# A new order of pieces with four places in a step, scores of one step in nine sent by pairs through the ring, and sums of values on column tiles

## The chip, the core and the metric

One core of a Trainium2 chip runs the whole program. The metric is the device time in microseconds (us), median of the runs shown. TensorE (PE), VectorE (DVE), ScalarE (ACT), GpSimd (POOL) and the DMA queue of SyncE (SP) work side by side and meet only at semaphores.

## The reference

The input x is 8 batches x 1024 tokens x 256 features, in fp32. Each batch goes through

```python
h = layernorm(x) * (1 + ca) + sa
x = x + ga * attention(h)        # 16 heads of 16 features
h = layernorm(x) * (1 + cb) + sb
x = x + gb * spikes(relu(h @ W_fc.T) ** 2 @ W_proj.T)   # 1024 hidden features, 5 LIF steps
```

The attention has two softmaxes. The scores (1024 x 1024 for a head) are cut into blocks of 128 keys; a first softmax runs inside each block with the causal mask, and a second softmax runs over the whole row of the first one's results, in which the masked entries count as zero and so give exp(0) = 1. The kernel therefore adds to each output the sum of the values of all later key blocks: this is the "sum of values" (pieces BH and BT below).

## The kernel before

**Steps.** The heads of a batch are taken four at a time (a group g), and a group in nine units of four PSUM banks, one for each head. The main loop has one step for each unit: 8 batches x 4 groups x 9 units = 288 steps and 14 more to drain. 36 steps make a period, which does the attention of one batch. Below, position p is the step's number modulo 36, and u = p modulo 9 the unit. Every engine runs the same steps in its own instruction order, written out in `step(n)` of that engine.

In step n PE does, in this order: `products` (second softmax times values, of step n - 7, L800), `sum_unit` (sums of the exponentials of step n - 1, L790), two `one_over_sums` (the inverse sums of step n - 5 spread over the partitions, L829), and the four `scores` (one for each head, L775, with a mask at L778), between which lie the tiles of maxima of the next group (`maxima`, L750 and L753), the pieces and the quanta. Step u = 0 has also `mixed_products`.

**PSUM.** Two banks `score0` and `score1` serve in turn the scores of each head, the pieces and the turned maxima: an item waits until the item before it in its bank has been taken away, mostly by ACT. Two double banks, the ring, serve in turn the two `one_over_sums` of a step, the maxima and the outputs; DVE takes these. One bank holds the sums, one the products.

**ACT** in a step: the second exponential of step n - 6 (L1046), every third step a logarithm and an exponential of sums (L1052, L1056), then the first exponentials of the four heads (L1041) with the evacuations of pieces (`take`) between them. **DVE**: every third step of nine an addition into `o_t` (L1196), two products with the inverse sums (L1180), every third step the inverse (L1184, L1186), then the maxima (L1158), after the last of a group a cast and a subtraction (L1172, L1174), layer norm statistics (L1132). After that PE turns the maxima (L763), ACT copies them (L1032), and SP loads them beside the queries with four DMAs (L554). **POOL**: split of the inverse sums (L1488 to L1494), split of queries and keys into three bf16 parts (L1454 to L1458), squares (L1467), LIF counts (L1475 to L1481), and the second half of each layer norm. **SP** stores the parts (L535), and loads the stacked parts of a whole group (L546) when step u = 0 is issued, in one order for all of it.

**Pieces.** Everything else of a batch is cut into pieces with a step and a place each, in hand-written tables: `FRONT` for the next batch (T1: transposes of the normalised input, QK: queries or keys, V: values, BH and BT: sum of values), `BACK` for the batch before (AT, O, T2, F1), `QUANTA` for single products with W_proj (L732, two instructions each). A piece at place 0 follows the score of head 0, at place 1 that of head 3. `TILES_AT` says how many maxima tiles a unit holds (three in each of u = 1 to 6).

**BH** does seven products of 8 columns of weights with 272 columns of values, all into the same 8 partitions of PSUM (L697, 14 instructions as fp32 takes two), ACT copies 8 x 272 numbers (L998), and **BT** turns them with four transposes (L702).

Of the kernel before, what the change touches and what calls it, by code (L numbers as in the profile page):

```python
# [5 lines left out]
F32 = mybir.dt.float32  # L6
# [7 lines left out]
P = 128  # L14
# [40 lines left out]
LAG_R, LAG_E, LAG_P = 5, 6, 7  # L55
LAST = NUNIT + 14
# [7 lines left out]
for _h in range(QH):  # L64
# [7 lines left out]
TILES_AT = {1: 3, 2: 3, 3: 3, 4: 3, 5: 3, 6: 3}  # L72
# [9 lines left out]
FRONT = {(2, 1): ('T1', 0), (1, 0): ('T1', 1), (1, 1): ('T1', 2), (5, 0): ('T1', 3), (3, 1): ('QK', 0), (5, 1): ('QK', 1), (6, 0): ('QK', 2), (13, 0): ('QK', 3), (15, 0): ('QK', 4), (16, 1): ('QK', 5), (17, 0): ('QK', 6), (15, 1): ('V', 0), (19, 1): ('QK', 7), (24, 0): ('V', 1), (21, 1): ('V', 2), (29, 0): ('V', 3), (30, 0): ('BH', 0), (31, 0): ('BT', 0)}  # L82
BACK = {(8, 0): ('AT', 0), (8, 1): ('AT', 1), (9, 0): ('AT', 2), (12, 0): ('AT', 3), (10, 0): ('O', 0), (11, 0): ('O', 1), (12, 1): ('O', 2), (14, 0): ('O', 3), (18, 0): ('T2', 0), (18, 1): ('T2', 1), (20, 1): ('T2', 2), (24, 1): ('T2', 3), (19, 0): ('F1', 0), (20, 0): ('F1', 1), (21, 0): ('F1', 2), (23, 0): ('F1', 3), (26, 1): ('F1', 4), (27, 0): ('F1', 5), (27, 1): ('F1', 6), (28, 0): ('F1', 7), (32, 0): ('F1', 8), (32, 1): ('F1', 9), (33, 0): ('F1', 10), (35, 0): ('F1', 11), (38, 0): ('F1', 12), (39, 0): ('F1', 13), (40, 0): ('F1', 14), (40, 1): ('F1', 15)}
# [3 lines left out]
QUANTA = {22: (3, 1, 0, 0), 23: (0, 0, 1, 1), 25: (1, 0, 2, 0), 26: (0, 2, 3, 0), 28: (0, 1, 0, 1), 29: (1, 1, 1, 2), 31: (2, 1, 1, 2), 32: (1, 0, 1, 0), 34: (1, 1, 1, 0), 35: (0, 1, 1, 2), 37: (1, 1, 0, 1), 38: (2, 0, 3, 0), 41: (1, 2, 0, 2), 43: (2, 2, 0, 0), 44: (1, 0, 1, 1), 36: (0, 0, 0, 1), 42: (0, 0, 2, 0), 30: (0, 0, 1, 0), 24: (0, 0, 1, 1), 45: (0, 0, 0, 1), 40: (1, 0, 0, 0)}  # L87


NEAR = {(39, 0): ("F1", 12), (39, 1): ("F1", 13), (41, 0): ("F1", 14), (41, 1): ("F1", 15)}  # L90
NEAR_QUANTA = {36: (0, 0, 0, 1), 37: (1, 1, 0, 1), 38: (2, 0, 3, 0), 42: (2, 2, 2, 2), 43: (2, 2, 2, 2)}
LATE = {(2, 0): ("AT", 0), (2, 1): ("AT", 1), (4, 0): ("O", 0), (4, 1): ("O", 1), (8, 0): ("AT", 2), (8, 1): ("AT", 3),
        (9, 0): ("T2", 0), (9, 1): ("T2", 1), (10, 0): ("O", 2), (10, 1): ("O", 3), (11, 0): ("F1", 0), (11, 1): ("F1", 1),
        (12, 0): ("F1", 2), (12, 1): ("F1", 3), (13, 0): ("F1", 4), (13, 1): ("F1", 5)}
# [4 lines left out]
    (2, 0): ("V", 0, 2), (2, 1): ("V", 0, 3), (6, 1): ("BH", 0, 0), (7, 1): ("BT", 0, 0),  # L99
    (10, 0): ("T1", 1, 0), (10, 1): ("T1", 1, 1), (11, 0): ("T1", 1, 2), (11, 1): ("T1", 1, 3),  # L100
# [5 lines left out]
FIRST[25, 0] = ("BH", 1, 0)  # L106
FIRST[26, 0] = ("BT", 1, 0)
# [9 lines left out]
def placed(n):  # L117

    out = [None, None]
    b, at = divmod(n, PERIOD)  # L120
    for k in range(2):
# [96 lines left out]

RING_NO = {}
for _k in range(BEGIN_TILES):  # L220
    RING_NO["m", 0, _k] = len(RING_NO)
for _n in range(LAST):
    if 0 <= _n - LAG_R < NUNIT:
        for _k in range(2):
            RING_NO["r", _n - LAG_R, _k] = len(RING_NO)
    for _g, _k in tiles_of(_n):
        RING_NO["m", _g, _k] = len(RING_NO)
    if turned_out(_n):
        RING_NO["o", turned_out(_n)[0], int(turned_out(_n)[1][0] > 0)] = len(RING_NO)

# [34 lines left out]

def score_slots():
# [3 lines left out]
    for n in range(LAST):  # L270
        p = placed(n)
        st = [("st", n, hh) for hh in range(QH)] if n < NUNIT else [None] * QH
        turn = ("turn", *turn_of(*turns(n))) if turns(n) else None
        begin = [p[0], st[0]] if piece_first(n) else [st[0], p[0]]
        steps.append([*begin, st[1], st[2], st[3], p[1], turn] if late_turn(n) else [*begin, st[1], turn, st[2], st[3], p[1]])
# [22 lines left out]
C_ID, C_MQ, C_MT, C_SEL, C_DS, C_U, C_AB, C_OH = 0, 128, 256, 384, 390, 428, 444, 448  # L298
# [3 lines left out]
def constants():  # L302
# [12 lines left out]
    c[:, C_U:C_U + NB - 1] = 1.0  # L315
    for j in range(NB):
        for row in (KROWS + 2 * j, KROWS + 2 * j + 1):
            c[row, C_OH + P * j:C_OH + P * (j + 1)] = 1.0
# [32 lines left out]
def build(nc, x, wqT, wkT, wvT, woT, bq, bk, bv, bo, wfcT, wprojT, cT, wmod, consts, out):  # L351
# [4 lines left out]
    with ExitStack() as ctx:  # L356
# [34 lines left out]
        b_out = sb("b_out", [P, 2 * D], BF16)  # L391
# [122 lines left out]

        block = ctx.enter_context(nc.Block())
# [3 lines left out]
        def _(sp):  # L519
# [123 lines left out]
        def _(pe):  # L643
# [11 lines left out]
            def ring_slot(*item):  # L655
                no = RING_NO[item]
                if no >= 2:
                    pe.wait_ge(ring_free, no - 1)
# [8 lines left out]
            def tokens_by(ps, src, n, w, bias=None):  # L667

                if bias is not None:
                    pe.matmul(ps, one[:, :].to_broadcast([P, P]), bias[:, :], start=True, stop=False, skip_group_check=True)  # L670
# [6 lines left out]
            def piece(item):  # L677
# [15 lines left out]
                elif kind == "BH":  # L693

                    piece_done(pe, "V", r, 3)
                    for j in range(1, NB):
                        mm = pe.matmul(ps[own_rows, 0:H * VW], u_ind[:, NB - 1 - j:2 * NB - 1 - j], v1[:, r % 2, j, :, :].rearrange("p h c -> p (h c)"),  # L697
# [870 lines left out]
```

## Time and profile before

| | |
|---|---|
| time, median of 3 runs | 2356.11 us (2353.27 to 2359.1) |
| profiled execution, its own time | 2358.39 us |
| span of its instructions | 2356.6 us |
| PE busy | 2206.2 us (94%) |
| DVE busy | 1753.1 us (74%) |
| ACT busy | 1541.6 us (65%) |
| POOL busy | 1137.6 us (48%) |
| mean granted PE clock | 0.990 |

The span lies 1.8 us under the execution's own time. Busy time is the union of an engine's instructions; a PE instruction counts as busy from its start to the modelled end of its result, so that neighbours overlap: the distance between two starts says what an instruction costs.

### The profile page before, as it was taken

To read this page: it belongs to the slowest core of one execution; us is meant where nothing else is said; L and a number is where in the kernel's file an instruction comes from. 1 tells how busy PE (TensorE), PEld (TensorE's weight loads), DVE (VectorE), ACT (ScalarE), POOL (GpSimd) and SP (SyncE) were. 2 spreads that over 40 slices of the span, in tenths; PEclk is the share of its full clock that TensorE was granted. 3 is DMA by queue.
4 is the path that set the end of the run, shared out by engine and by line. 5 is a ranking of instruction groups with operands and counts; after the bars stand their busy time and mean duration, and the time that the engine had idled before them with its cause. 6 is when DMAs were issued, how large, how long until landed. Compare 5 with 4: busy or idle time off the path is not lost.

```text
span 2356.6 us, 46649 instructions
## 1 busy us (share of the span) xinstructions
PE 2206.2 (94%) x19164; PEld 1247.1 (53%) x19164; DVE 1753.1 (74%) x2115; ACT 1541.6 (65%) x2157; POOL 1137.6 (48%) x1070
## 2 busy tenths in 40 slices
PE   6889889999999999999998999999999999989988
PEld 4434334455555555455554655545555555545557
DVE  7786887768787676886778777776877767788466
ACT  2477677766667667676777766776666766667741
POOL 3153133545755456644576257653576544443630
PEclk9999999999999999999999999999999999999999
DMA  5233122311122113121133102231022211101000
GB/s 188 62 109 94 48 55 71 94 48 33 54 68 84 52 35 90 41 68 52 35 90 95 47 20 59 66 108 48 8 70 77 84 35 46 39 19 29 6 27 25
DMA packets 114064, 140.20 MB, mean 59 GB/s; under 512 B 8648, under 2 KB 86760, under 8 KB 113856
## 3 DMA queue, kind: packets, MB, share of 16 engines
q1 hardware_dynamic: 113856, 137.23, 20.5%
q8 instruction: 155, 2.54, 0.5%
q14 instruction: 53, 0.43, 0.1%
HBM read 74.26 MB, written 58.74 MB: 56 GB/s over the span
## 4 chain that ended last, share of the span: by engine, by line
PE 77%; DVE 10%; ACT 5%; POOL 4%; issue 2%; DMA 1%; SPq 0%; ACTq 0%; POOLq 0%
PE pv L800 11%; PE ring L750 9%; PE sums L790 9%; PE score L775 9%; PE score L720 9%; PE sums L732 8%; PE score L673 5%; PE score L688 4%; DVE e L1180 4%; PE ring L829 4%; DVE negmax L1158 3%; PE ring L753 2%; PE score L778 2%; PE score L664 2%; ACT e L1041 2%
## 5 line engine op out<-in xcount | busy, mean ns | idle before, releaser
L1041 ACT ACTIVATE e<-score 128x512 f32<-128x512 f32 x1152 | 672.7, 595 | 372.8 <-PE score L778 207.6
L1180 DVE TENSOR_TENSOR e<-ring,e 128x1024 f32<-128x1024 f32 x576 | 681.2, 1224 | 278.1 <-PE ring L829 277.5
L1158 DVE TENSOR_REDUCE negmax<-ring 128x8 f32<-128x1024 f32 x576 | 681.7, 1219 | 150.7 <-PE ring L753 139.4
L1046 ACT ACTIVATE e<-e 128x2048 f32<-128x2048 f32 x288 | 548.6, 1905 | 4.9 <-DVE e L1180 4.9
L775 PE MATMUL score<-q_st,k_st 112*128 112x512 bf16 (+3 forms) x1536 | 459.5, 330 | 57.3 <-ACT e L1041 22.5
L750 PE MATMUL ring<-k_st,q_st 96*128 96x512 bf16 (+3 forms) x1664 | 387.5, 318 | 39.1 <-DVE e L1180 18.1
L1488 POOL TENSOR_SCALAR r_p<-r_b,ab 128x256 bf16<-128x256 f32 x96 | 89.6, 934 | 544.5 <-DVE r_b L1186 544.5
L800 PE MATMUL pv<-e,v 128*17 128x512 f32 (+3 forms) x3072 | 314.4, 497 | 1.3 <-DVE o_t L1196 1.3
L790 PE MATMUL sums<-e,d_ones 128*32 128x256 f32 x4608 | 305.1, 383 | 1.4
L775 PEld LDWEIGHTS score<-q_st,k_st 112*128 112x128 bf16 x1536 | 147.9, 97 | 248.9 <-issue 122.7
L1467 POOL TENSOR_TENSOR gT<-gT 128x512 f32<-128x512 f32 x112 | 117.2, 1051 | 331.5 <-ACT gT L1014 331.5
L732 PE MATMUL sums<-w_proj,gT 128*128 128x256 f32 x896 | 259.3, 394 | 8.1 <-POOL gT L1467 3.7
L720 PE MATMUL score<-hT,w_fc 128*128 128x256 f32 x1024 | 244.2, 383 | 2.7 <-ACT e L1041 1.4
L790 PEld LDWEIGHTS sums<-e,d_ones 128*32 128x32 f32 x4608 | 147.6, 111 | 179.4 <-issue 96.9
L750 PEld LDWEIGHTS ring<-k_st,q_st 96*128 96x128 bf16 x1664 | 150.1, 99 | 147.4 <-DVE negmax L1158 42.4
L753 PE MATMUL ring<-mask_q,id_b 128*128 128x128 bf16 x1024 | 221.5, 221 | 0.0
L720 PEld LDWEIGHTS score<-hT,w_fc 128*128 128x128 f32 x1024 | 189.7, 190 | 33.2 <-ACT e L1041 6.3
L778 PE MATMUL score<-id_b,mask_q 128*128 128x128 bf16 x1024 | 192.3, 220 | 0.0
L732 PEld LDWEIGHTS sums<-w_proj,gT 128*128 128x128 f32 x896 | 148.5, 191 | 38.7 <-DVE r_b L1184 6.6
L1479 POOL TENSOR_SCALAR below<-n 128x512 bf16<-128x512 f32 x104 | 154.9, 1490 | 7.4
L1014 ACT ACTIVATE gT<-score 128x512 f32<-128x512 f32 x112 | 66.9, 597 | 123.4 <-PE score L720 123.4
L753 PEld LDWEIGHTS ring<-mask_q,id_b 128*128 128x128 bf16 x1024 | 100.3, 98 | 53.6 <-issue 3.5
(147 smaller groups left out, 2574.9 us busy)
## 6 DMA issues: line engine op xcount, KB each, us to landing
q_st<-q_parts SPq DMA_DIRECT2D x31, 768.0 KB, 5.9
k_st<-k_parts SPq DMA_DIRECT2D x31, 768.0 KB, 8.6
q_parts<-qk_p SPq DMA_DIRECT2D x30, 384.0 KB, 2.6
k_parts<-qk_p SPq DMA_DIRECT2D x28, 384.0 KB, 2.6
x_in<-in_x SPq DMA_DIRECT2D x8, 1024.0 KB, 5.7
q_parts<-qk_p SPq DMA_DIRECT2D x30, 256.0 KB, 2.9
x_res<-in_x SPq DMA_DIRECT2D x30, 256.0 KB, 4.1
k_parts<-qk_p SPq DMA_DIRECT2D x28, 256.0 KB, 2.9
```

Source lines behind the costliest of these rows:

```text
L720: mm = pe.matmul(ps[:, HALF * i:HALF * i + HALF], w_fc[:, k, P * f:P * f + P], (last_h if r == LB else hT2)[:, k, HALF * c:HALF * c + HALF ...
L732: mm = pe.matmul(sums[:, HALF:HALF + D], gT[:, f, P * i:P * i + P], w_proj[:, f, :], start=(n > NUNIT and f == 0), stop=(f == NF - 1), ski ...
L750: mm = pe.matmul(slot[:, c:stop], q, k_st[0:KROWS, g % 2, hh, c + shift:stop + shift], start=True, stop=not own, skip_group_check=True)
L753: mm = pe.matmul(slot[:, diag:diag + P], id_b[:, :], mask_q[:, :], start=False, stop=True, skip_group_check=True)
L775: mm = pe.matmul(slot[:, c:c + qb - qa], k_st[0:KROWS + MROWS, g % 2, hh, P * j:P * j + P], q_st[0:KROWS + MROWS, g % 2, hh, qa:qb], start ...
L778: mm = pe.matmul(slot[:, c:c + P], mask_q[:, :], id_b[:, :], start=False, stop=True, skip_group_check=True)
L790: mm = pe.matmul(sums[32 * hh:32 * hh + 32, 0:HALF], d_ones[:, 2 * TRI - 1 - row:2 * TRI + 31 - row], e[:, m % ES, hh, HALF * c:HALF * c + ...
L800: mm = pe.matmul(pv[32 * hh:32 * hh + VW, qa - at:qb - at], v1[:, b % 2, j, QH * g + hh, :], e[:, m % ES, hh, c:c + qb - qa], start=start, ...
L1041: act.activation(e[:, n % ES, hh, :], score[SCORE_SLOT["st", n, hh][0]][:, :], ACT.Exp, scale=DK ** -0.5).then_inc(e1_done, 1)
L1046: act.activation(v, v, ACT.Exp).then_inc(e2_done, 1)
L1158: dve.tensor_reduce(negmax[:, hh:hh + heads, at:at + NB // heads], slot[:, :].rearrange("p (h a n) -> p h a n", h=heads, n=P), AX_X, ALU.m ...
L1180: dve.tensor_tensor(v, ring[no % 2][:, :].rearrange("p (i n) -> p i n", i=2), v, ALU.mult).then_inc(ring_free, 1)
```

## The change

- `placed` gives four places, one behind the score of each head, and `FRONT`, `BACK` and `QUANTA` are new. `TILES_AT` has two tiles at u = 3 and four at u = 4.
- In the 31 steps with u = 0 that hold no tiles (`paired`) the scores of heads 0 and 1 go into one double bank of the ring, those of heads 2 and 3 into the other, and ACT takes each with one exponential of 1024 columns. Places 0 and 1 then lie ahead of the scores, place 2 between the pairs, place 3 behind them. The two score banks serve only pieces there.
- BH writes its seven products to four groups of 32 partitions in turn, with 32 columns of weights; ACT copies 128 x 272 numbers into `o_t`; BT is 16 small products (17 columns of weights, 8 of data) instead of four transposes. DVE's write to `o_t` waits for BT.
- The bias of the output projection is made once and read twice, which takes one DVE instruction off the start.

```diff
-TILES_AT = {1: 3, 2: 3, 3: 3, 4: 3, 5: 3, 6: 3}
+TILES_AT = {1: 3, 2: 3, 3: 2, 4: 4, 5: 3, 6: 3}
-FRONT = {(2, 1): ('T1', 0), (1, 0): ('T1', 1), (1, 1): ('T1', 2), (5, 0): ('T1', 3), (3, 1): ('QK', 0), (5, 1): ('QK', 1), (6, 0): ('QK', 2), (13, 0): ('QK', 3), (15, 0): ('QK', 4), (16, 1): ('QK', 5), (17, 0): ('QK', 6), (15, 1): ('V', 0), (19, 1): ('QK', 7), (24, 0): ('V', 1), (21, 1): ('V', 2), (29, 0): ('V', 3), (30, 0): ('BH', 0), (31, 0): ('BT', 0)}
+FRONT = {(0, 0): ('T1', 0), (0, 1): ('T1', 1), (5, 2): ('T1', 2), (1, 3): ('T1', 3), (0, 3): ('QK', 0), (5, 3): ('QK', 1), (6, 0): ('QK', 2), (13, 3): ('QK', 3), (15, 0): ('QK', 4), (15, 2): ('QK', 5), (17, 0): ('QK', 6), (16, 3): ('V', 0), (19, 3): ('QK', 7), (24, 0): ('V', 1), (18, 2): ('V', 2), (29, 0): ('V', 3), (35, 0): ('BH', 0), (35, 3): ('BT', 0)}
-BACK = {(8, 0): ('AT', 0), (8, 1): ('AT', 1), (9, 0): ('AT', 2), (12, 0): ('AT', 3), ..., (12, 1): ('O', 2), ..., (24, 1): ('T2', 3), ..., (35, 0): ('F1', 11), ...}
+BACK = {(9, 0): ('AT', 0), (8, 0): ('AT', 1), (12, 3): ('AT', 2), (12, 0): ('AT', 3), ..., (13, 0): ('O', 2), ..., (22, 3): ('T2', 3), ..., (33, 2): ('F1', 11), ...}
-QUANTA = {..., 25: (1, 0, 2, 0), 26: (0, 2, 3, 0), ..., 29: (1, 1, 1, 2), 31: (2, 1, 1, 2), ..., 42: (0, 0, 2, 0), 43: (2, 2, 0, 0), 44: (1, 0, 1, 1), 45: (0, 0, 0, 1), 30: (0, 0, 1, 0), ...}
+QUANTA = {..., 25: (1, 2, 1, 1), 26: (1, 0, 2, 0), ..., 29: (0, 1, 0, 0), 31: (2, 3, 2, 0), ..., 42: (0, 0, 1, 0), 43: (1, 1, 1, 0), 44: (2, 1, 1, 1), 30: (0, 0, 0, 3), ...}
+def paired(n):
+    return n % NU in PAIRED and n < NUNIT and not tiles_of(n)
...
                 elif kind == "BH":
                     piece_done(pe, "V", r, 3)
                     for j in range(1, NB):
-                        mm = pe.matmul(ps[own_rows, 0:H * VW], u_ind[:, NB - 1 - j:2 * NB - 1 - j], v1[...], start=(j == 1), stop=(j == NB - 1))
+                        own = slice(32 * (j % 4), 32 * (j % 4) + 32)
+                        mm = pe.matmul(ps[own, 0:H * VW], u_ind[:, NB - 1 - j:NB + 31 - j], v1[...], start=(j <= 4), stop=(j >= 4), skip_group_check=True)
                 elif kind == "BT":
                     for g in range(NQ):
-                        mm = pe.transpose(ps[:, NB * g:NB * g + NB], suf_t[...], id_f[own_rows, own_rows])
+                        for hh in range(QH):
+                            mm = pe.matmul(ps[32 * hh:32 * hh + VW, NB * g:NB * g + NB], suf_p[:, QH * g + hh, 0:VW], eight[:, :], start=True, stop=True, skip_group_check=True)
...
+                if paired(n):
+                    if p[1]:
+                        piece(p[1])
+                    for item in single[0]:
+                        quantum(n, *item)
+                    scores(n, 0)
+                    scores(n, 1)
...
+                    if p[2]:
+                        piece(p[2])
...
+                    scores(n, 2)
+                    scores(n, 3)
+                    if p[3]:
+                        piece(p[3])
...
+            def paired_exp(n, pair):
+                no = RING_NO["s", n, pair]
+                act.wait_ge(ring_ready, no + 1)
+                act.activation(e[:, n % ES, 2 * pair:2 * pair + 2, :], ring[no % 2][:, :].rearrange("p (i n) -> p i n", i=2), ACT.Exp, scale=DK ** -0.5).then_inc(e1_done, 2)
```

## Rows read from the trace of the kernel before

**Rows 1.** Windows: span, busy us of PE, PEld, DVE, ACT, POOL, clock, DMA.

```profile
1145.83:1426.43 280.60, 270.66 (x2391) 153.96 (x2391) 211.71 (x247) 192.82 (x271) 157.16 (x146) 1.00 0.21 60
...
1237.16:1273.02 35.86, 32.60 (x278) 16.08 (x277) 33.19 (x39) 24.46 (x34) 25.21 (x24) 1.00 0.13 42
1378.72:1395.33 16.61, 16.61 (x129) 7.99 (x129) 13.84 (x17) 9.80 (x16) 3.83 (x5) 1.00 0.05 17
```

**Rows 2.** Groups by line: busy us, mean ns, idle before, releasers.

```profile
L1158 DVE TENSOR_REDUCE negmax<-ring 128x8 f32<-128x1024 f32 x576 | 681.7, 1219 | 150.7 <-PE ring L753 139.4 <-PE ring L750 8.7
L1180 DVE TENSOR_TENSOR e<-ring,e 128x1024 f32<-128x1024 f32 x576 | 681.2, 1224 | 278.1 <-PE ring L829 277.5
L1041 ACT ACTIVATE e<-score 128x512 f32<-128x512 f32 x1152 | 672.7, 595 | 372.8 <-PE score L778 207.6 <-PE score L775 142.9
L1046 ACT ACTIVATE e<-e 128x2048 f32<-128x2048 f32 x288 | 548.6, 1905 | 4.9 <-DVE e L1180 4.9
L775 PE MATMUL score<-q_st,k_st 112*128 112x512 bf16 (+3 forms) x1536 | 459.5, 330 | 57.3 <-ACT e L1041 22.5 <-ACT qk_p L992 18.8 <-ACT m_sb L1032 9.4
```

**Rows 3.** Timeline, PE, position 0: around the score of head 2.

```profile
1148.64 0.22 PE L778 MATMUL score<-id_b,mask_q 128*128 128x128 bf16 x1
1149.45 0.38 PE L775 MATMUL score<-q_st,k_st 112*128 112x512 bf16 x1 [0.58 <-ACT e L1041]
```

**Rows 4.** Timeline, PE, positions 18 and 27: around the same kind of wait.

```profile
1288.31 0.22 PE L778 MATMUL score<-id_b,mask_q 128*128 128x128 bf16 x1
1288.87 0.38 PE L775 MATMUL score<-q_st,k_st 112*128 112x512 bf16 x1 [0.35 <-ACT hT L974]
...
1357.08 0.22 PE L778 MATMUL score<-id_b,mask_q 128*128 128x128 bf16 x1
1357.88 0.38 PE L775 MATMUL score<-q_st,k_st 112*128 112x512 bf16 x1 [0.58 <-ACT e L1041]
```

**Rows 5.** Timeline, DVE, position 0: the products that free the ring.

```profile
1147.68 2.35 DVE L1180 TENSOR_TENSOR e<-ring,e 128x1024 f32<-128x1024 f32 x2 [0.17 <-PE ring L829]
```

**Rows 6.** Chain of waits at positions 30 and 31: start, us, what.

```profile
1381.29 3.31 PE score L697 x14
...
1389.96 0.34 PE score L702 x4
```

**Rows 7.** Chain of waits: two `products`, one of 384 and 128 columns, one of 512.

```profile
1195.57 0.99 PE pv L800 x16
...
1203.56 0.98 PE pv L800 x8
```

**Rows 8.** Timeline, POOL: first split of QK1, last split of QK2.

```profile
1195.53 1.17 POOL L1454 TENSOR_TENSOR qk_p<-qk_f,qk_p 128x512 bf16<-128x512 f32 x1 [1.24 <-ACT qk_p L992]
...
1210.81 1.18 POOL L1458 TENSOR_TENSOR qk_p<-qk_f,qk_p 128x512 bf16<-128x512 f32 x1
```

**Rows 9.** Timeline, SP, and from the DMA view the last one's landing.

```profile
1212.02 2.76 SPq L535 DMA_DIRECT2D k_parts<-qk_p  x3
1214.82 2.39 SPq L554 DMA_DIRECT2D q_st<-m_sb  x4
1217.88 0.48 SPq L546 DMA_DIRECT2D k_st<-k_parts  x1
...
k_st<-k_parts SPq DMA_DIRECT2D x1, 768.0 KB, 8.8
```

**Rows 10.** Timeline, PE, position 10: the first tile of maxima.

```profile
1226.84 0.22 PE L750 MATMUL ring<-k_st,q_st 96*128 96x128 bf16 x1
```

**Rows 11.** Timeline, PE and DVE, position 16: the turn of the maxima.

```profile
1273.02 0.61 PE L763 MATMUL score<-id_b,maxp 128*64 128x128 bf16 x8 [1.53 <-DVE maxp L1174]
...
1271.25 1.62 DVE L1174 TENSOR_TENSOR maxp<-negmax,maxp 128x168 bf16<-128x168 f32 x1
```

**Rows 12.** Timeline, PE, position 17: a score behind a QK piece.

```profile
1283.91 0.34 PE L775 MATMUL score<-q_st,k_st 112*128 112x384 bf16 x1 [1.02 <-ACT qk_p L992]
```

**Rows 13.** Timeline, DVE, the start: the bias, made twice.

```profile
38.85 2.55 DVE L1352 TENSOR_TENSOR b_out<-e 3x256 bf16<-3x256 f32 x2
```

More of the change, by code:

```diff
@@ L55 @@
 LAG_R, LAG_E, LAG_P = 5, 6, 7
+PAIRED = (0,)
 LAST = NUNIT + 14
@@ L117, in placed @@
 def placed(n):
-    out = [None, None]
+    out = [None] * 4
     b, at = divmod(n, PERIOD)
-    for k in range(2):
+    for k in range(4):
         if b == 0 and (at, k) in FIRST:
@@ L216, in turned_out, with last_turned, last_summed @@
     return None
+PIECE_STEP = {piece: n for n in range(LAST) for piece in placed(n) if piece}
+def last_turned(n):
+    done = [turned_out(k)[0] for k in range(n) if turned_out(k)]
+    return done[-1] if done else None
+def last_summed(n):
+    done = [r for r in range(B) if PIECE_STEP["BT", r, 0] < n]
+    return done[-1] if done else None
+def paired(n):
+    return n % NU in PAIRED and n < NUNIT and not tiles_of(n)
 RING_NO = {}
@@ L227 @@
         RING_NO["m", _g, _k] = len(RING_NO)
+    if paired(_n):
+        for _k in range(2):
+            RING_NO["s", _n, _k] = len(RING_NO)
     if turned_out(_n):
         RING_NO["o", turned_out(_n)[0], int(turned_out(_n)[1][0] > 0)] = len(RING_NO)
+RING_ITEM = list(RING_NO)
+FREE_NO = {item: k for k, item in enumerate(item for item in RING_ITEM if item[0] != "s")}
 def turns(n):
@@ L263, in piece_first @@
     return mixed(n) or n == max(BEGIN_AT) + 1
+ST_NO = [QH * sum(not paired(k) for k in range(n)) for n in range(NUNIT)]
 def score_slots():
@@ L271, in score_slots @@
         p = placed(n)
-        st = [("st", n, hh) for hh in range(QH)] if n < NUNIT else [None] * QH
+        st = [("st", n, hh) for hh in range(QH)] if n < NUNIT and not paired(n) else [None] * QH
         turn = ("turn", *turn_of(*turns(n))) if turns(n) else None
+        if paired(n):
+            steps.append([p[0], p[1], turn, p[2], p[3]])
+            continue
         begin = [p[0], st[0]] if piece_first(n) else [st[0], p[0]]
-        steps.append([*begin, st[1], st[2], st[3], p[1], turn] if late_turn(n) else [*begin, st[1], turn, st[2], st[3], p[1]])
+        steps.append([*begin, st[1], p[1], *([] if late_turn(n) else [turn]), st[2], p[2], st[3], p[3], *([turn] if late_turn(n) else [])])
     steps.append(TAIL)
@@ L315, in constants @@
     c[:, C_U:C_U + NB - 1] = 1.0
+    for i in range(NB):
+        c[i::32, C_8 + i] = 1.0
     for j in range(NB):
@@ L669, in tokens_by @@
                 if bias is not None:
-                    pe.matmul(ps, one[:, :].to_broadcast([P, P]), bias[:, :], start=True, stop=False, skip_group_check=True)
+                    pe.matmul(ps, one[:, :].to_broadcast([P, P]), bias[:, :].unsqueeze(1).to_broadcast([P, 2, D]), start=True, stop=False, skip_group_check=True)
                 for i in range(2):
@@ L879, in step @@
             def step(n):
-                first, second = placed(n)
+                p = placed(n)
                 single = quanta(n)
@@ L901, in step @@
                     scores(n, 0)
-                if first and not piece_first(n):
-                    piece(first)
+                if p[0] and not piece_first(n):
+                    piece(p[0])
                 for item in single[0]:
@@ L923, in step @@
                     maxima(*at[2])
-                if second:
-                    piece(second)
+                if p[3]:
+                    piece(p[3])
                 if 3 in at:
@@ L1077, in step @@
                 b, s = divmod(n, PERIOD)
-                first, second = placed(n)
+                p = placed(n)
                 t = n // TRI - 1
@@ L1195, in take_products @@
                     dve.wait_ge(ring_ready, RING_NO["o", g - 1, 0] + 1)
+                if half == 0 and last_summed(n) is not None:
+                    piece_full(dve, "BT", last_summed(n), 0)
                 dve.tensor_tensor(o_t[:, BANK * half:BANK * half + BANK].rearrange("p (i n) -> p i n", n=P),
@@ L1382, in step @@
                     invert(t)
-                first, second = placed(n)
-                if first and first[0] == "O":
-                    take_output(first)
+                p = placed(n)
+                for item in p[:2]:
+                    if item and item[0] == "O":
+                        take_output(item)
                 tiles = tiles_of(n)
@@ L1388, in step @@
                     maxima(g, k)
-                if second and second[0] == "O":
-                    take_output(second)
+                for item in p[2:]:
+                    if item and item[0] == "O":
+                        take_output(item)
                 if turned_out(n):
```

192 lines of the change are left out of this document (131 added, 61 removed).

## The prediction

> **What bounds the kernel now.** I read the busy times first: PE 270.7 of the 280.6 us of a period, DVE 211.7, ACT 192.8, POOL 157.2 [rows 1]. PE paces the whole, yet not alone: since all 36 positions repeat to 0.01 us from batch to batch, I went through one period start by start. Summing the distances between PE starts and setting against them what each kind of instruction takes when nothing holds it leaves about 26 us per period beyond the work, of which 11 are small gaps of 0.1 us (some three a step, an estimate that I take as unavoidable), and 15 are real waits. The change can give back only these 15 and whatever PE work it removes. Where the 15 lie:
>
> - Positions with u = 0: 1.2, 1.0, 1.2 and 1.3 us. The four scores share two banks, so the third waits for the exponential of the first: from the mask at 1148.64 to the next score at 1149.45 are 0.81 us where 0.06 would do [rows 3]; positions 18 and 27 show 0.56 and 0.80 [rows 4], each with smaller ones behind.
> - Positions 12 to 16: 4.6 us up to the turn of the maxima. From the start of step 12 to the turn are 35.86 us, and DVE is busy in 33.2 of them [rows 1]: two products and three tiles of 1.22 us a step [rows 2], with outputs, statistics and the cast on top. The turn waits 1.5 us for DVE's last subtraction [rows 11].
> - A score that needs the bank of a QK piece, which ACT empties with two instructions: 1.0 us at position 17 [rows 12], the like at 6 and 13, and 1.2 us at 16 behind the copy of the turned maxima.
> - Positions 33 to 35: 1.8 us, DVE again.
>
> **BH and BT.** Fourteen instructions take 3.31 us on PE [rows 6], 0.236 each, as all write the same 8 partitions. On four groups of 32 partitions at most two products (four instructions) share a group: 4 x 0.236 = 0.94. The nearest row says that groups do overlap: `products` takes 0.98 us for eight instructions of 512 columns over four such groups [rows 7]. That saves 2.4 us; the bounds are 0 (no overlap) and 2.5 (3.31 / 4). BT was 0.34 us for four transposes [rows 6]; now it is 32 instructions. Sixteen instructions, eight of 384 and eight of 128 columns, take 0.99 us, and eight of 512 take 0.98 [rows 7]; at three quarters of that the first eight cost 0.74, which leaves 0.25 for the other eight, 0.031 each, with 17 columns of weights like BT's. 32 x 0.031 = 1.0 us. From the transposes (0.34 / 4 = 0.085 each) it would be 2.7; the low bound is the 0.34 of before. I take 1.0, since the 17 columns of weights are the same. Net 1.7 us for a batch; the bounds are a gain of 2.5 (full overlap, BT as before) and a loss of 2.4 (no overlap, BT at 2.7). Six batches have it on PE's path: 10.2 us. The first period computes two more in steps where DVE sets the pace, of which I count half: 1.7 us. Sum 11.9 us.
>
> TensorE's floor for small matmuls speaks against BT: the Trainium skill ("TensorE: Matmul & The Clock Gate", section "Wait — 56ns, not 53.3ns?") gives about 62 ns for a matmul when the sequencer decodes in software, and about 25 ns otherwise. With 62 BT would take 2.0 us and the net saving shrink from 1.7 to 0.7 us a batch; the 0.031 worked out from the products [rows 7] disagrees with 62 and fits 25.
>
> **The paired scores.** Their exponential of 1024 columns: 595 ns for 512 and 1905 for 2048 [rows 2] give 0.853 ns a column, so 1.03 us, 0.16 less than two. ACT is not the bound, so this counts only through waits. What counts is when the ring is free: the first pair needs DVE's first product (ends near 1148.9), the second pair the second (1150.03) [rows 5]. At position 0, PE would reach the scores at 1148.1; T1 0 and T1 1 (0.44 each) now lie ahead of them and carry it to 1149.0, so the first pair runs at once, to 1149.6; the second waits until 1150.1, 0.5 us; QK0 follows behind it. Waits 1.2 before, 0.6 after. At 18, V2 (1.7 us) lies between the pairs and covers the second product: 1.2 to 0.2. At 27, F1 5 (1.7 us) lies ahead: 1.3 to 0.1. At 9 only AT 0 is there: some 0.5 remains, and the next `sum_unit` waits for the exponential of the second pair.
>
> **Positions 6 to 10: a chain that PE doesn't set.** The first split of QK1 starts at 1195.53, at the head of step 6, and POOL works without a gap to 1211.99 through it, the last LIF count, the gate and residual, the inverse sums and QK2 [rows 8]. Behind it SP, in its own order, issues QK2's stores, the four loads of maxima, then the stacks, the last at 1217.88, landing 8.8 us later at 1226.7; PE's first tile from that stack starts at 1226.84 [rows 9, 10]. So this stretch of 31.3 us is as long as POOL, SP and DMA make it, and PE stands at its edge already. The change takes 0.9 us of PE work out of it (AT 2 leaves, one quantum net leaves) and moves QK1's evacuation 0.4 us later against the head of step 6. The queue's content is the same. Nothing is won by the pairs at 9, and the waits grow from 2.0 to 3.1.
>
> **Positions 12 to 16.** DVE's load there is the same: one tile moves from 12 to 13, O2 too. AT 2 fills 0.4 us of the wait. Against it, V0 (one evacuation) changes places with QK5, and QK5 now lies ahead of the last two tiles, which so reach DVE close together; walked through step by step, DVE ends its subtraction about 1 us later. Waits 4.6 to 5.1. POOL's QK5 split now comes directly behind QK4's, and SP stores QK5 ahead of the loads of maxima: these land some 3 us before the scores of 18 need them, so I count nothing; without that cover every us would count one. The waits behind the turn at 16 and behind QK6 at 17 stay at 2.3.
>
> **Positions 29 to 35.** BH, which DVE used to catch up, leaves position 30: 3.3 us less, while DVE has 6.5 us of work in it (two products, two tiles, inverse, two statistics) and then four tiles. It was busy in 13.8 of 16.6 us of steps 30 and 31 [rows 1]; these shrink to about 15. Walked through, the ring holds PE 1.4 us at 30: 0.2 to 1.5. F1 11 between the pairs of tiles at 33 and the earlier square at 35 give 1.8 to 1.0. Other positions (2 and 4 tiles at 3, 4, 21, 22; more quanta at 25) 0.2 to 0.4.
>
> **Sum for a period.** Before 1.2 + 2.0 + 4.6 + 2.3 + 1.2 + 1.3 + 0.2 + 1.8 + 0.2 = 14.8; after 0.6 + 3.1 + 5.1 + 2.3 + 0.2 + 0.1 + 1.5 + 1.0 + 0.4 = 14.3. That is 0.5 x 6 = 3 us in six periods. The seven paired steps of the first and last period give 0.6 each, 4 us. The bias is costed at nothing: one of two DVE instructions of together 2.55 us goes [rows 13], but the first tiles wait for their stacks' DMAs there; at most 1.3. In all 11.9 + 3 + 4 = 19 us off the profiled execution's 2358.4, which is 2.3 above the median: 2356 - 19 = 2337 us. As my walks round every wait up, I put the forecast at 2336.
>
> **The rivals.**
> 1. *The order fits* (0.2). Neither DVE nor the stack chain binds as I have it: then the waits of 6 to 16 fall by what the pairs save and those of 29 to 31 stay at 0.2: 14.8 - 4 = 10.8 a period, 24 + 4 + 11.9 = 40 us, 2316. For it: POOL is idle in much of the period; against it: DVE's 33.2 of 35.9.
> 2. *Small matmuls and no overlap eat BH's gain* (0.1). BT at 2.7 us leaves nothing of it: 7 us off, 2349; without overlap too, a loss of 2 us a batch, 2362.
> 3. *The pairs stall PE as much as the banks did* (0.1): the first pair waits for DVE, the next sums for a whole exponential of 1.03. Then only BH's 11.9 remain less 3 to 8 us: 2348 to 2353.
> 4. *Slower* (0.1). The store of QK5 ahead of the loads of maxima: QK5's split takes three POOL instructions of 1.17 and its three stores 2.76 [rows 8, 9], 6.3 us in a row ahead of the loads, of which my walk finds room for all and 3 us more. If the maxima land later than that by x, every period loses x: from x = 19 / 6 = 3.2 us the gain is gone, and with x = 5 it is 30 us lost, 2367.
>
> **How the numbers follow.** Forecast's own case 0.5, with 2325 to 2346. The measurement can tell about 0.3% (7 us) from no change. Faster than 2349: 0.5 + 0.2 + half of the rivals 2 and 3 = 0.78. Within 7 us: 0.11. Slower: 0.11. The range from 2308 to 2356 holds the own case, rivals 1 and 3 and half of 2.
>
> **What would show it.** BH near 0.9 and BT near 1.0 us on PE; at positions 0, 18, 27 no score waiting for an exponential, but a 0.5 us wait for DVE's second product at 0; the first tile of position 10 waiting for the stack's DMA; step 30 at 6.9 us with a ring wait; the turn at 16 some 2 us late. The forecast is wrong if the stacks land earlier than 31 us behind QK1's split, if DVE is idle in 12 to 16, or if the scores of 18 wait for their maxima.

## The result and the profile after

The changed kernel takes 2348.4 us (median of 10 runs, 2343.01 to 2350.09) against 2357.9 for the kernel before (10 runs beside it, 2353.27 to 2359.6). The ratio is 0.9957, 95% interval 0.9948 to 0.9967: 9.5 us or 0.43% faster, beyond the 0.3% that can be told from no change. The forecast was 20 us, 2336. Direction and range held (2308 to 2356); the size was more than twice what came.

The page of the changed kernel (busy us and share of the span of 2346.9 us, instructions); against it stand 2206, 1753, 1542 and 1138 us in the table of before:

```profile
PE 2189.8 (93%) x19388; PEld 1252.1 (53%) x19388; DVE 1759.8 (75%) x2115; ACT 1535.1 (65%) x2095; POOL 1133.4 (48%) x1070
```

PE lost 16 us of work and the span only 10. The windows of the same batch as in [rows 1], of its position 0, and of 3.45 us inside position 0 (columns as there; the clock is the last but two):

```profile
1139.34:1420.20 280.86, 268.94 (x2437) 154.97 (x2424) 213.25 (x247) 191.95 (x263) 156.34 (x146) 0.99 0.21 60
1139.34:1150.21 10.87, 8.56 (x88) 4.10 (x72) 7.73 (x9) 6.88 (x10) 10.44 (x11) 0.84 0.71 170
1144.15:1147.60 3.45, 3.45 (x20) 1.77 (x20) 2.92 (x4) 1.78 (x3) 3.45 (x4) 0.52 1.04 246
```

The period is 280.86 us where it was 280.60: in the middle of the program the change gives nothing at all. Laid beside each other start by start (the first from its step 1 on), the eight periods differ by -3.1, -4.5, then +0.3, +0.1, +0.3, +0.1, +0.4 and at last -2.7 us; the drain behind them gives -1.2 and the start-up +0.8. All the gain is at the two ends.

So the question is what eats BH and BT's saving in each period of the middle. I set the 36 step lengths of this batch beside those of before. Thirty-five of them together are shorter by 5.4 us; position 0 is longer by 5.65. Of this some 2.9 is work that was moved there (T1 0 0.58, T1 1 0.49 and QK0 1.77, by the distances between starts in a run below where nothing holds them), and 2.8 is waiting and work stretched by a lower clock. PE in position 0 of the changed kernel:

```profile
1139.12 0.38 PE L755 MATMUL score<-eight,o_t 128*17 128x8 f32 x32
1139.34 0.67 PE L862 MATMUL pv<-e,v 128*17 128x256 f32 x8
1139.88 1.07 PE L852 MATMUL sums<-e,d_ones 128*32 128x256 f32 x16
1140.89 0.40 PE L891 MATMUL ring<-r_p,sel 32*128 32x256 bf16 x8
1143.60 0.63 PE L714 MATMUL score<-id_f,x_in 128*128 128x128 f32 x4 [2.31 <-DVE x_in L1416]
1144.15 0.99 PE L862 MATMUL pv<-e,v 128*17 128x256 f32 x8
1145.07 1.12 PE L714 MATMUL score<-id_f,x_in 128*128 128x128 f32 x4
1145.98 0.63 PE L834 MATMUL ring<-q_st,k_st 112*128 112x512 bf16 x1
1146.41 0.31 PE L837 MATMUL ring<-id_b,mask_q 128*128 128x128 bf16 x1
...
1147.58 0.44 PE L834 MATMUL ring<-q_st,k_st 112*128 112x512 bf16 x1
```

T1 0 (L714) stands idle for 2.31 us, waiting for DVE's normalised input. Behind the wait the same score takes 0.63 us where it took 0.38 [rows 3]: in these 3.45 us the granted clock is 0.52, the lower of its two levels (1.2 GHz), until it is back to full at 1147.6. DVE and POOL at the same time:

```profile
1138.75 4.70 DVE L1416 TENSOR_SCALAR x_in<-x_in,mv,rstd 128x256 f32<-128x256 f32 x4
1143.37 0.68 DVE L1332 TENSOR_TENSOR o_t<-pv,suf 128x512 f32<-128x512 f32 x1
1143.97 2.34 DVE L1314 TENSOR_TENSOR e<-ring,e 128x1024 f32<-128x1024 f32 x2
```

```profile
1139.45 1.17 POOL L1618 TENSOR_TENSOR acc<-acc,below 128x512 f32<-128x512 f32 x1
1140.69 1.27 POOL L1669 TENSOR_TENSOR acc<-acc,gates 128x512 f32<-128x512 f32 x1
1142.04 1.26 POOL L1671 TENSOR_TENSOR acc<-acc,x_res 128x512 f32<-128x512 f32 x1
```

One by one, the four DVE tiles run 1138.75-1139.51, 1139.43-1140.76, 1140.69-1142.11 and 1142.03-1143.45. Each of the last three starts together with a POOL instruction and ends 0.15 us behind it. With POOL idle as the tile starts it takes 0.41 us (23 records of this trace, 0.406 to 0.415). Over the whole trace the wait has this one source (PE, idle before T1, by releaser):

```profile
L714 PE MATMUL score<-id_f,x_in 128*128 128x128 f32 x256 | 44.1, 304 | 13.0 <-DVE x_in L1416 12.7 <-ACT hT L1097 0.2
```

The same trace holds a control. At position 0 of the second batch no batch has come to its spike counts yet, so POOL runs none of the three additions. There the four tiles take 1.61 us, T1 0 waits 0.57 us, the clock stays at full, and the step takes 8.01 us in place of 10.87 (0.5 of this is a quantum that it doesn't have). DVE, POOL and PE there:

```profile
308.55 1.61 DVE L1416 TENSOR_SCALAR x_in<-x_in,mv,rstd 128x256 f32<-128x256 f32 x4
308.62 5.03 POOL L1582 TENSOR_SCALAR x_in<-x_in,mv,rstd 128x256 f32<-128x256 f32 x4 [11.38 <-DVE rstd L1285]
310.31 0.63 PE L714 MATMUL score<-id_f,x_in 128*128 128x128 f32 x4 [0.57 <-DVE x_in L1416]
```

The kernel before was not free of the lower clock either, and the prediction overlooked it: its positions do not all repeat to 0.01 us, since position 16 takes 9.49 us in four of six batches and 11.19 in two (with the half clock behind its waits). Between 300 and 1960 us the clock record of the trace has three such stretches before, and seven after the change: five at position 0 and two at 16.

### The profile page after: what moved, and what is told of

The parts are those of the page before. It is cut to its first block, busy times and chain, and to the rows that moved or that the text cites. A ratio compares the mean times of both kernels' runs of the same rounds, so it can differ in the third digit from the quotient of the medians.

```text
span 2346.9 us, 47050 instructions
## 1 busy us (share of the span) xinstructions
PE 2189.8 (93%) x19388; PEld 1252.1 (53%) x19388; DVE 1759.8 (75%) x2115; ACT 1535.1 (65%) x2095; POOL 1133.4 (48%) x1070
## 4 chain that ended last, share of the span: by engine, by line
PE 76%; DVE 17%; ACT 3%; issue 2%; DMA 1%; SPq 0%; POOL 0%; ACTq 0%
PE pv L862 10%; PE score L774 10%; PE sums L852 9%; PE ring L804 9%; PE sums L786 8%; PE score L834 8%; DVE e L1314 6%; DVE negmax L1292 5%; PE score L723 5%; PE ring L891 4%; PE score L738 3%; PE ring L807 2%; PE score L837 2%; DVE x_in L1416 2%; PE score L714 1%
## 5 line engine op out<-in xcount | busy, mean ns | idle before, releaser
L1134 ACT ACTIVATE e<-score 128x512 f32<-128x512 f32 x1028 | 604.2, 595 | 375.3 <-PE score L837 207.0
L834 PE MATMUL score<-q_st,k_st 112*128 112x512 bf16 (+3 forms) x1412 | 413.8, 326 | 34.0 <-ACT qk_p L1082 15.8
L834 PEld LDWEIGHTS score<-q_st,k_st 112*128 112x128 bf16 x1412 | 135.9, 98 | 175.2 <-issue 61.0
L837 PE MATMUL score<-id_b,mask_q 128*128 128x128 bf16 x900 | 165.5, 220 | 0.0
```

Of the source, the lines that this page charges most:

```text
L834: mm = pe.matmul(slot[:, c:c + qb - qa], k_st[0:KROWS + MROWS, g % 2, hh, P * j:P * j + P], q_st[0:KROWS + MROWS, g % 2, hh, qa:qb], start ...
L837: mm = pe.matmul(slot[:, c:c + P], mask_q[:, :], id_b[:, :], start=False, stop=True, skip_group_check=True)
L1134: act.activation(e[:, n % ES, hh, :], score[SCORE_SLOT["st", n, hh][0]][:, :], ACT.Exp, scale=DK ** -0.5).then_inc(e1_done, 1)
```

## The experiments

Theory A, formed from these rows: T1 0 at the head of position 0 needs DVE's normalisation, which ends late because POOL holds it up, and the half clock that follows the wait adds to it. Rival B: the position is long because of what was moved into it and because of the ring, and T1 only happens to stand where the wait shows. Rival C: the new order is the loss and the pairs give nothing. The comparison kernel took 2356.4 to 2358.2 us in these sessions; ratios are against it. Differences from the changed kernel are between medians of different sessions and can be off by some 2 us.

**One part: the sums of values alone.** The old tables, with BH and BT of the new form at position 35, and no step in pairs.

```diff
-PAIRED = (0,)
+PAIRED = ()
-FRONT = {(0, 0): ('T1', 0), ..., (35, 0): ('BH', 0), (35, 3): ('BT', 0)}
+FRONT = {(2, 3): ('T1', 0), ..., (35, 1): ('BH', 0), (35, 3): ('BT', 0)}
```

> The old tables of pieces, quanta and tiles and no paired step; of the change only the sums of values on four groups of partitions (BH at place 1, BT at place 3 of position 35, as they now use the output buffer) and the bias made once. Theory A (the gain of the changed kernel, about 10 us, is all from BH and BT, and the new order gives back what the pairs save): BH about 0.95 us and BT 0.22 us on PE instead of 3.31 and 0.34, 2.4 us less work a batch, and the DVE-bound steps 30 and 31 give a third of it back: 10 to 16 us faster than before, so at or under the changed kernel's time. Rival B (BH's removal from position 30 is worthless, since DVE sets the pace there): within 4 us of before.

Measured: 2350.58 us (5 runs), ratio 0.997, interval 0.9957 to 0.9983. That is 7 us, less than theory A's 10 to 16 and more than rival B's 4. Most of it is again not from the middle: a period is 280.3 us, 0.3 less than before where both run at full clock, though PE has 2.4 us less to do. Where they went is in step 30, which BH has left:

```profile
1371.42 0.61 PE L834 MATMUL score<-q_st,k_st 112*128 112x512 bf16 x2
1372.80 0.23 PE L804 MATMUL ring<-k_st,q_st 96*128 96x128 bf16 x1 [0.77 <-DVE e L1314]
...
1375.85 0.60 PE L804 MATMUL ring<-k_st,q_st 96*128 96x512 bf16 x2 [0.60 <-DVE negmax L1292]
```

Before, step 30 took 8.67 us with hardly a wait, 5.36 without BH; now it takes 7.21, since waits for the ring, which DVE empties, are some 1.8 us longer. BH was a pause in which DVE caught up. Position 35 grew by 1.6 us with the new BH and BT in it, and step 31 lost 0.45.

**The same with pairs.** The kernel of the last run with `PAIRED = (0,)`, still in the old order.

> As the kernel with the sums of values alone, and with the paired scores in the steps u = 0, still with the old tables. Theory A: the pairs save 0.9 us at 18 and 1.3 at 27 and about nothing at 0 and 9, where the second pair waits for DVE's second product (no piece lies between): 2 us a period, 12 to 16 us faster than the kernel with the sums alone. Rival B (pairs only move the wait from the score bank to the ring): within 4 us of it.

Measured: 2348.75 us (10 runs), 0.9962, 0.9951 to 0.9974. Beside the last kernel: position 27 -1.36 us, 18 -0.42, 9 and 10 +0.2, 0 and 1 +0.5, together -1.05 a period; in some periods 1.7 came back at position 16 as a half clock. By the time, 1.8 us less than the last kernel, rival B's 4 us hold and theory A's 12 to 16 do not: position 27 gave what was expected, 18 half of it, and positions 0, 1 and 10 and the clock took most of it back. So the old order with both other parts is as fast as the whole change (2348.4): the new order adds nothing. Whether it has any part in the gains of the edits further down is open, since they were not run in the old order.

**The new order without pairs.** The changed kernel with `PAIRED = ()`.

> The changed kernel without a paired step: the new tables, scores by heads everywhere. Theory A (pairs are worth 1 to 2 us a period, at 18 and 27): 7 to 14 us slower than the changed kernel. Rival B (the new order has put pieces where they cover the score bank's waits too, so that pairs are worth nothing): within 4 us of it. At position 0 the four scores then don't wait for the ring, but T1 0 and DVE's lateness stay.

Measured: 2369.24 us (4 runs), 1.0052, 1.0037 to 1.0067. It is slower than the kernel before, and 21 us slower than with pairs; no theory had more than 14. Positions 18 and 27 lose 1.37 and 1.36 us, as expected. Position 0 loses 2.24, because there T1 1 and the second half of the scores now wait for one another's banks (start, us, PE):

```profile
1153.64 0.63 PE L714 MATMUL score<-id_f,x_in 128*128 128x128 f32 x4 [2.31 <-DVE x_in L1416]
...
1156.18 1.12 PE L714 MATMUL score<-id_f,x_in 128*128 128x128 f32 x4 [0.24 <-ACT e L1134]
...
1158.26 0.58 PE L834 MATMUL score<-q_st,k_st 112*128 112x512 bf16 x1 [0.43 <-ACT hT L1064]
1158.64 0.31 PE L837 MATMUL score<-id_b,mask_q 128*128 128x128 bf16 x1
1158.74 3.39 PE L738 MATMUL score<-hT,w_q 128*128 128x512 f32 x4
```

The 2.31 us before T1 0 are the same to 0.01, so the pairs have no part in that wait. The lower clock now lasts through QK0 (3.39 us, 1.93 in the changed kernel), and position 16 gains one too (+1.68). Of rival C one half holds and one falls. Without pairs the new order is a loss, 18.7 us beside the old order without pairs (2350.58). But the pairs are worth 21 us in it and 2 in the old order. That this is because the order puts pieces into the paired steps, ahead of or between the scores, is read from positions 0, 18 and 27 and not tested by itself.

**T1 out of position 0.** T1 0 to 3 and QK0 back at the steps they had.

```diff
-FRONT = {(0, 0): ('T1', 0), (0, 1): ('T1', 1), (5, 2): ('T1', 2), (1, 3): ('T1', 3), (0, 3): ('QK', 0), ...
+FRONT = {(2, 3): ('T1', 0), (1, 0): ('T1', 1), (1, 3): ('T1', 2), (5, 0): ('T1', 3), (3, 3): ('QK', 0), ...
```

> The changed kernel with T1 0, T1 1 and QK0 taken out of position 0 (to 2, 1 and 3, T1 2 and T1 3 to 1 and 5, as before). Theory A (DVE is late at position 0: its four normalisations take 4.7 us against POOL and end 4.1 us into the step, and everything of DVE behind them is late too): the wait of 2.4 us at T1 0 goes, but the first pair of scores then waits for DVE's first product until about 5.9 us into the step; step 0 lasts 7.5 to 8.5 us with over 2.5 us of waits, and the kernel stays within 8 us of the changed one. Rival B (only the piece at the head is wrong, being put ahead of its data): the waits of step 0 fall to 1.2 us and the kernel is 15 to 25 us faster than the changed one.

Measured: 2355.7 us (10 runs), 0.9985, 0.9972 to 0.9998; 7 us slower than with T1 in position 0. Seven of the ten executions took 2354.8 to 2360.1 us at mean granted clocks of 0.981 to 0.984, and three 2347.6 to 2348.7 at 0.988 and 0.989, as fast as the changed kernel: so the 7 us come and go with the clock, and what is shown is that the kernel got no faster. The trace is of the slowest. In it step 0 has 2.8 us less work, takes 9.24 us (7.5 to 8.5 expected) and is only 1.64 shorter. The wait didn't go; it stands one instruction further on:

```profile
1148.11 0.41 PE L891 MATMUL ring<-r_p,sel 32*128 32x256 bf16 x8
1151.34 1.06 PE L862 MATMUL pv<-e,v 128*17 128x256 f32 x8 [2.82 <-DVE o_t L1332]
1152.56 0.58 PE L834 MATMUL ring<-q_st,k_st 112*128 112x512 bf16 x1 [0.17 <-DVE e L1314]
```

`mixed_products` waits for DVE's addition into `o_t`, and that stands behind the normalisation in DVE's order, as do the products that free the ring. So it isn't T1's place that costs: whatever PE does there waits for the same four DVE instructions. So theory A as it stood at the head of this section needed mending: the cause is DVE's lateness, T1 is only the first to meet it. Rival B of this run (15 to 25 us faster) falls.

**POOL taken away beside the normalisation.** The LIF counts of one of the two chunks of a step on POOL run on 1 column in place of 512, so that POOL has done its adds before DVE normalises. The spikes of that chunk are so counted for one column alone (the diff shows one of three instructions).

```diff
+                    w = 1 if c == 1 else BANK
-                    pool.tensor_scalar(acc[:, :], n1[:, :], -levels[k], None, ALU.is_lt)...
+                    pool.tensor_scalar(acc[:, 0:w], n1[:, 0:w], -levels[k], None, ALU.is_lt)...
```

> The changed kernel with POOL's spike counts of the second chunk of each batch cut to one column (that chunk's output is left wrong). Theory A (DVE's normalisations at the end of position 35 take 1.2 us each instead of 0.41 because POOL works on the same memory port in turn): they fall to 0.4 to 0.6 us each, end within 1.5 us of the head of step 0, the wait of T1 0 goes and with it the half clock behind it: 3 us a period or more, 18 to 28 us faster than the changed kernel. Rival B (DVE starts them too late by its own order): they stay over 3 us together or T1 0 still waits over 1.5 us, under 8 us faster.

Measured: 2330.52 us (4 runs), 0.9889, 0.9874 to 0.9904: 18 us less than the changed kernel, the low edge of what theory A expected, by taking work from an engine that is busy 48% of the time. Each period gives back 3.6 us, and all of it lies in position 0 (10.88 to 7.33; the other positions move by at most 0.12). DVE and PE there:

```profile
1132.60 1.62 DVE L1416 TENSOR_SCALAR x_in<-x_in,mv,rstd 128x256 f32<-128x256 f32 x4
```

```profile
1135.24 0.41 PE L891 MATMUL ring<-r_p,sel 32*128 32x256 bf16 x8
1135.58 0.66 PE L714 MATMUL score<-id_f,x_in 128*128 128x128 f32 x4
1136.16 0.63 PE L862 MATMUL pv<-e,v 128*17 128x256 f32 x8
1136.72 0.66 PE L714 MATMUL score<-id_f,x_in 128*128 128x128 f32 x4
1137.21 0.38 PE L834 MATMUL ring<-q_st,k_st 112*128 112x512 bf16 x1
```

The normalisation takes 1.62 us in place of 4.70 and starts 1.09 us ahead of the step in place of 0.59, T1 0 waits for nothing, and the clock stays at full. So of the 3.6 us that it ends earlier 3.1 are the shorter run and 0.5 an earlier start. Of the 3.55 us of the step 2.4 are the wait and 1.2 the lower clock, which had stretched the work behind the wait by 1.6 and covered 0.4 of waiting for the ring. Rival B falls: with the same pieces in the same places only that wait of 0.4 us, ahead of the third score, is left.

**The normalisation one step earlier.** No work is left out. DVE does Newton's step and two of the four tiles at step 34 and the other two at 35, ACT's guess moves from 34 to 33.

```diff
-                    normalise(r, range(4), x_in, mv1, rstd1, newton1, xn1[0])
+                    normalise(r, range(2), x_in, mv1, rstd1, newton1, xn1[0])
+                elif k == 6:
+                    normalise(r, range(2, 4), x_in, mv1, rstd1, newton1, xn1[0])
...
+                if b + 2 < B and s == 34:
+                    first_norm(n, b + 2, 5)
-                    first_norm(n, b + 2, {28: 0, 29: 1, 30: 2, 31: 3, 33: 4, 35: 5}.get(s))
+                    first_norm(n, b + 2, {28: 0, 29: 1, 30: 2, 31: 3, 32: 4, 35: 6}.get(s))
-                if s == 34 and b + 2 < B:
+                if s == 33 and b + 2 < B:
```

> The changed kernel with DVE's own half of the next batch's normalisation split and moved: aggregation at position 32 instead of 33, the rest's first guess at 33 instead of 34, Newton step and two tiles at 34 ahead of the division, two tiles at 35. POOL's work stays whole. Theory A (T1 0 and DVE's products wait at position 0 because DVE's four tiles, slowed by POOL, all lie behind the products of 35): step 0 falls from 10.9 to under 8 us, the half clock at its end goes, and the kernel is 14 to 22 us faster than the changed one, near the one with POOL's counts short, unless the tiles at 34 delay the outputs (then 8 to 14). Rival B (POOL's load itself holds PE back elsewhere, as by late squares or inverse sums): step 0 falls but other steps lengthen, under 6 us faster.

Measured: 2337.51 us (4 runs), 0.9913, 0.9896 to 0.9931, 11 us less than the changed kernel. Theory A had expected 14 to 22 us. Position 0 gives the same 3.55 us and 35 takes 0.42 back; position 34, where theory A feared a delay of the outputs, is unchanged. But in this batch 1.32 come back at position 16, where no instruction was touched:

```profile
1264.01 0.61 PE L817 MATMUL score<-id_b,maxp 128*64 128x128 bf16 x8 [1.42 <-DVE maxp L1308]
...
1265.79 0.61 PE L834 MATMUL score<-q_st,k_st 112*128 112x512 bf16 x1 [0.79 <-ACT m_sb L1125]
...
1266.30 3.08 PE L723 MATMUL score<-w_v,hT 128*128 128x256 f32 x7
```

The turn waits 1.42 us for DVE and a score 0.79 for ACT's copy, as in the changed kernel; what is new is that the clock falls to its lower level behind them. It fell so in four of the six batches of the middle, where it had in two of the changed kernel. It is that which hid a part of the gain.

**V0 between the score and the turn.** In position 16 V0 moves from place 3 to place 1, ahead of the turn.

```diff
-(16, 3): ('V', 0)
+(16, 1): ('V', 0)
```

> The changed kernel with V0 at place 1 instead of 3 of position 16, ahead of the turn of the maxima that waits 1.6 us for DVE. Theory A (DVE's maxima chain sets the turn, PE's piece behind it finds nothing else to fill the wait): the wait falls to zero and step 16 from 9.39 to about 7.9 us, 8 to 10 us faster than the changed kernel, with fewer stretches of half clock. Rival B (what lies behind the turn is late in its place: the copy of the turned maxima, the score behind it and the outputs): the step stays over 9 us, under 3 us faster.

Measured: 2339.74 us (4 runs), 0.9927, 0.9911 to 0.9944, 9 us less than the changed kernel, as theory A expected. The step takes 8.37 us (some 7.9 expected, but V0 itself now waits 0.47 us for its bank). That is 1.0 us less in each period, and in every second one some 1.5 more go, which were a half clock: all periods now take 279.9 us (280.9 and 282.4 in turn in the changed kernel).

```profile
1264.75 1.99 PE L723 MATMUL score<-w_v,hT 128*128 128x256 f32 x8 [0.47 <-ACT e L1134]
1266.68 0.63 PE L817 MATMUL score<-id_b,maxp 128*64 128x128 bf16 x8
```

**Together.** First both edits and two quanta moved (one from position 6 to 7, one within 34); then both edits alone.

```diff
-34: (1, 2, 1, 0), ..., 42: (0, 0, 1, 0)
+34: (2, 1, 1, 0), ..., 42: (0, 1, 0, 0)
```

> The changed kernel with the normalisation moved as in the first of this call, V0 ahead of the turn, and one quantum each moved ahead of a wait (position 42 from place 2 to 1, position 34 from place 1 to 0). Theory A (the waits are separate and each is worth what it measures): 3.5 us a period from step 0, 1.5 from 16, 0.4 from 6 and 0.4 from 34, 28 to 36 us faster than the changed kernel, 2312 to 2322. Rival B (DVE's load sets the sum, and what one place gives the next takes back): 12 to 20 us faster.

> The two edits of norm_early (half of the first layer norm of the next batch one step earlier) and v0_ahead_of_turn (V0 at place 1 of position 16) together, with the quanta where the change has them. Against the changed kernel norm_early took some 11 us off and v0_ahead_of_turn some 9. Theory A (the two act at different places, 0 and 16, and the half clock does not come back elsewhere): the sum or a little more, 2323 to 2331 us, because norm_early alone had moved half-clock stretches to position 16, which V0's place takes away. Rival B (the combined version's 26 us came in good part from moving the quanta from 6 to 7 and within 34): 2332 to 2338, no better than the better one of the two by more than 5 us.

Measured: 2322.6 us (4 runs), 0.9855, 0.984 to 0.987; and without the quanta 2322.81 us (4 runs), 0.9866, 0.9846 to 0.9886. The intervals overlap: the two edits give the gain, and the quanta nothing that these runs can tell. By position each takes 0.4 us out of its own step and puts 0.4 into the next (6 and 7, 34 and 35). 25.6 us is more than the 20 of the two runs alone, as each edit removes the half clock that the other's kernel still had. The window of the batch, and of position 0:

```profile
1125.00:1401.85 276.85, 267.92 (x2444) 154.30 (x2430) 212.54 (x246) 191.73 (x263) 157.00 (x146) 1.00 0.22 61
1125.00:1132.33 7.33, 7.08 (x90) 3.35 (x74) 3.92 (x5) 6.62 (x10) 7.09 (x7) 1.00 0.82 196
```

In these traces no stretch at the half clock is left between 300 and 1960 us without the quanta, and one with them. With nothing left out, this version is 1.3% faster than the kernel before and some 1% faster than the change. The first run fell short of its theory A (25.8 us gained, 28 to 36 expected); its rival's account of the two quanta was right. The second came out at the edge of theory A (2322.81, 2323 to 2331 expected), and its rival, that the quanta brought the rest, falls.

## Why the prediction was right and where it was wrong

Per period of the middle I had forecast -0.5 us of waiting and -1.7 of work, and it came to +2.4 to 2.7 and -2.4. By its steps (waits by position are distances between starts less what the same work takes elsewhere, good to some 0.3 us):

- **The step that failed** is that of the paired scores at position 0: "T1 0 and T1 1 (0.44 each) now lie ahead of them and carry it to 1149.0, so the first pair runs at once". It costed T1 as work, and took its input as being there. Waits were to fall from 1.2 to 0.6; they rose to 4.0, the lower clock's 1.6 included, which no term of the sum had. That is 3.4 us a period too little, in five middle periods 17 us. (The 0.44 had no row either: the two take 0.58 and 0.49.) The row that would have shown it lies just ahead of those I read of DVE [rows 5]. Its normalisation in the kernel before:

```profile
1144.20 2.71 DVE L1280 TENSOR_SCALAR x_in<-x_in,mv,rstd 128x256 f32<-128x256 f32 x4
```

  It ended at 1146.91, 1.08 us into the step, and T1 0, behind `one_over_sums`, would have asked for it at about 1147.6: 0.7 us to spare. In the changed kernel it ends 4.11 into the step. Of the 3.0 us between, 1.0 is a later start beside PE's (position 35 takes 6.46 us and not 7.82, as F1 11 left it and the new BH and BT are short) and 2.0 a longer run (4.70 in place of 2.71), since POOL now runs three TENSOR_TENSOR beside it and not one. I had asked of each moved piece what bank it needs, and of this one not who makes its input.
- **BH and BT** gained more than forecast: BH 3.31 to 1.04 us (0.94 forecast), BT 0.34 to 0.22 (1.0 forecast), 2.4 us in place of 1.7. The Trainium skill ("TensorE: Matmul & The Clock Gate", section "Wait — 56ns, not 53.3ns?") gives about 25 ns as the least for a matmul; here 32 of them start within 0.22 us, 6.9 ns apart, on four groups of columns. Every fourth of them starts 25 ns after. So as a least for any two matmuls this trace disagrees with it; as a least for two of the same group it would fit, but the rows don't name the group. The prediction's 0.031 had come from matmuls of 128 columns of data [rows 7], where BT's have 8. Rival 2 is out.
- **Positions 18 and 27** lost 0.94 and 1.36 us of waiting, together 2.3 us (2.2 forecast). The score banks' waits have gone, as rival 3 would not have it; that the time, 2348.4 us, lies at the edge of rival 3's 2348 to 2353 is chance.
- **Positions 6 to 10**: +0.7 (+1.1 forecast). The reason given was the wrong one: the stack was issued at 1214.52 and landed 8.5 us later at 1223.0, and PE's first tile came at 1223.58. So the sign named for this step, the first tile waiting for the DMA, did not come: the stack landed 30.0 us behind the first split of QK1 (1192.99), not 31, which the prediction had called a sign of being wrong, and the DMA was 0.6 us away from binding. That the size came out near is luck; the waits of 9 and 10 are for the ring, which DVE empties, and for the exponential of 1024 columns.
- **Positions 12 to 17**: +0.7 where 0.5 was forecast; DVE sets their pace, and at 13 it lost 0.86 us when one inverse took 1.28 beside a POOL addition in place of 0.42.
- **Step 30** took 6.81 us with a wait of 1.50, forecast 6.9 and 1.5. Positions 29 to 31 rose by some 0.6 to 0.9 (1.3), 33 to 35 fell by 0.5 to 0.7 (0.8), and 1, 22 and 32 rose by 0.5 each, where I had 0.2 for all such.
- **Rival 4** did not come: SP's six stores took 5.58 us from 1271.19, the loads of maxima followed at 1276.82, and the scores of 18 waited for DVE alone.
- **The ends** gave 10.8 us, the first two periods 7.6, the last 2.7 and the drain 1.2, less 0.8 of start-up, where the forecast left 8 for them (19 less five periods of 2.2). In the second period, without additions on POOL beside the normalisation, position 0 rose by 2.0 us only; a part of its 4.5 is a stretch at the half clock at position 7, which the kernel before had there and the changed one not.

The forecast of the middle periods without position 0 would have been right to 1.0 us (-1.6 forecast, -2.6 measured), most of it BH and BT, with errors of both signs in the rest. What stays open: why the clock fell in some of these steps and not in others with nearly the same waits (position 16 in every second period of the changed kernel). That two edits take it away is shown, not what sets it off.

## What to carry to other kernels

When a piece is moved to an earlier place, look up the engine that makes its input and what runs beside that engine at that time, before its banks: 0.7 us of slack was used up here by 1.0 us of faster PE and 2.0 of slower DVE. An edit that shortens PE can bring a wait into a step that was not touched, so compare step by step and not by totals. And after a wait was found, take out work beside the late engine once, as a test: it told cause from place in one run. An edit's gain can also be hidden by the granted clock in another step, so look at the clock of each step before an edit is given up.

## What the runs showed of the hardware

- **DVE beside POOL.** DVE's fp32 normalisation (128 x 256, SBUF to SBUF) took 0.41 us where POOL was idle 0.05 us after the tile's start (23 records of the changed kernel), 0.58 on the mean where it ran a TENSOR_SCALAR (14) and 1.35 where it ran a TENSOR_TENSOR (27). The inverse (L1320, two inputs) took 0.43, 0.43 and 1.21. The product that reads PSUM and SBUF took 1.22 to 1.23 beside all three. By the Trainium skill ("SBUF — State Buffer", section "Who interferes with whom") the two engines share a pair of ports, held by one instruction as a whole while the other waits, where DVE reads two inputs from SBUF or works in a mode that takes both ports. This trace agrees for POOL instructions with two inputs, though no run shows the mode that DVE was in. Beside POOL's with one input DVE was held up by 0.17 us on the mean, much less than a whole instruction of 1.5 us; the rule by itself would have it wait to the end.
- **The clock.** Behind a PE wait of 2.31 us the granted clock was 0.52 for 3.45 us; behind 1.42 and 0.79 us, close together, it fell in some periods and not in others, and where it fell position 16 took 11.07 us in place of 9.39. At position 0 the wait cost its own length and half as much again.
- **Small matmuls** (17 columns of weights, 8 of data) on four groups of columns start 6.9 ns apart on the mean (32 within 0.22 us). Matmuls of 272 columns took 1.04 us for 14 on four groups, and 3.31 on one.
